# Reordering the opening and the projection stage of a depool and feed-forward kernel

## What is computed

```python
h = rmsnorm(layernorm(x), g_res) @ W_in.T + b_in
c = rmsnorm(ctx, g_init)[:, :512]                # the mean square is over all 1024 columns
s[t] = a * s[t-1] + b * c[t]                     # a scan over the 3202 rows, a = 1 - exp(-0.001)
plug = clip(cumsum(boundary(cumsum(mask))) - 1, 0, 3201)
x1 = x + h + s[plug]
out = x1 + gelu(layernorm(x1) @ w1 + b1) @ w2 + b2    # w1 is 512 x 2048, w2 is 2048 x 512
```

## Time and profile before

| what | value |
|---|---|
| median of 3 runs (lowest to highest) | 852.49 us (850.71 to 853.28) |
| the profiled execution, its own time | 856.67 us |
| its span | 854.9 us |
| mean granted TensorE clock | 0.994 |
| TensorE matmuls busy | 835.0 us, 98% |
| VectorE, ScalarE, POOL busy | 322.9, 273.9, 251.5 us |
| chain that ended last | 90% TensorE, 3% VectorE, 2% ScalarE, 2% DMA |
| POOL, four low parts of w1 (128x512 each, L487, at 114.37) | 5.61 us |
| VectorE CAST of 128x26 at 43.40, beside a POOL product; another at 47.96, alone | 1.29 us, 0.18 us |

### The profile page before, as it was taken

The page is one execution under the profiler, slowest core; times in us unless marked ns, Lnnn a source line. Parts: engine busy times, 40 slices in busy tenths (PEclk is TensorE's granted clock), DMA queues, the critical chain, the costliest instruction groups (busy, mean ns, idle before and its releaser), DMA issues.

```text
span 854.9 us, 10715 instructions
## 1 busy us (share of the span) xinstructions
PE 835.0 (98%) x3766; PEld 683.4 (80%) x3766; DVE 322.9 (38%) x529; ACT 273.9 (32%) x482; POOL 251.5 (29%) x234
## 2 busy tenths in 40 slices
PE   5899999899999999999999999999999999999998
PEld 3688888688888888788888887888888888888886
DVE  4899972434333241424141424234113411241112
ACT  4173325542441235122622243213222222222221
POOL 0174176970163106220532034202500250011000
PEclk9899999999999999999999999999999999999999
DMA  9567698150213212150116021402300140010001
GB/s 241 173 177 241 208 257 308 50 155 17 74 49 108 63 50 74 51 119 9 64 68 151 0 74 49 97 0 74 74 1 1 49 87 11 0 49 1 1 1 49
DMA packets 34968, 71.07 MB, mean 83 GB/s; under 512 B 5716, under 2 KB 5716, under 8 KB 33176
## 3 DMA queue, kind: packets, MB, share of 16 engines
q1 hardware_dynamic: 25964, 58.91, 21.2%
q0 software_dynamic: 4608, 8.39, 6.1%
q10 hardware_dynamic: 4368, 3.42, 1.4%
HBM read 47.87 MB, written 22.84 MB: 83 GB/s over the span
## 4 chain that ended last, share of the span: by engine, by line
PE 90%; DVE 3%; ACT 2%; issue 2%; DMA 2%; POOL 0%; ACTq 0%; SPq 0%; DVEq 0%; POOLq 0%
PE acc L781 15%; PE acc L783 15%; PE acc L782 15%; PE h_bank L781 14%; PE h_bank L782 14%; PE h_bank L783 14%; PE t_bank L827 2%; DVE cl L949 2%; PE t_bank L769 1%; DMA ch<-in_ctx_dram 1%; PE acc L777 1%; DMA xa_even<-in_x_dram 1%; PE t_bank L800 1%; PE acc L769 0%; ACT g_f L721 0%
## 5 line engine op out<-in xcount | busy, mean ns | idle before, releaser
L1155 DVE TENSOR_TENSOR h_lo<-g_f,h_hi 128x512 fp32r<-128x512 f32 x128 | 99.6, 778 | 456.1 <-ACT g_f L721 456.1
L719 ACT ACTIVATE h_hi<-h_bank,b_c 128x512 fp32r<-128x512 f32 x128 | 88.1, 688 | 436.9 <-PE h_bank L783 432.0
L781 PE MATMUL h_bank<-xt_hi,w_hi 128*128 128x512 f32 x512 | 202.4, 395 | 0.0
L783 PE MATMUL h_bank<-xt_hi,w_lo 128*128 128x512 f32 x512 | 200.0, 391 | 0.0
L782 PE MATMUL h_bank<-xt_lo,w_hi 128*128 128x512 f32 x512 | 200.0, 391 | 0.0
L781 PE MATMUL acc<-w_hi,h_hi 128*128 128x512 f32 x512 | 199.8, 390 | 0.0
L783 PE MATMUL acc<-w_hi,h_lo 128*128 128x512 f32 x512 | 199.2, 389 | 0.0
L782 PE MATMUL acc<-w_lo,h_hi 128*128 128x512 f32 x512 | 199.2, 389 | 0.0
L781 PEld LDWEIGHTS h_bank<-xt_hi,w_hi 128*128 128x128 f32 x512 | 96.6, 189 | 21.0 <-issue 1.2
L782 PEld LDWEIGHTS h_bank<-xt_lo,w_hi 128*128 128x128 f32 x512 | 96.4, 188 | 20.9 <-issue 1.2
L783 PEld LDWEIGHTS h_bank<-xt_hi,w_lo 128*128 128x128 f32 x512 | 96.5, 189 | 20.3
(11 more groups left out here) (152 smaller groups left out, 687.8 us busy)
## 6 DMA issues: line engine op xcount, KB each, us to landing
out_dram<-x_cur SPq DMA_DIRECT2D x32, 256.0 KB, 2.1
x_next<-x_part SPq DMA_DIRECT2D x7, 1024.0 KB, 4.8
w_raw<-in_L_ffn_w_dram SPq DMA_DIRECT2D x6, 1024.0 KB, 9.8
scan_table<-cl SPq DMA_DIRECT2D x6, 896.0 KB
ch<-in_ctx_dram SPq DMA_DIRECT2D x20, 256.0 KB, 2.9
cl<-in_ctx_dram SPq DMA_DIRECT2D x5, 1024.0 KB
xa_even<-in_x_dram SPq DMA_DIRECT2D x16, 256.0 KB, 5.8
xa_odd<-in_x_dram SPq DMA_DIRECT2D x16, 256.0 KB, 6.7
```

Of the source, the lines that this page charges most:

```text
L719: act.activation(h_hi[:, m % HB, :], h_bank[m % 2][:], ACT.Gelu, bias=b1_c[:, m:m + 1])
L781: nc.tensor.matmul(dst, a_hi, b_hi, start=first, stop=False)
L783: return nc.tensor.matmul(dst, a_lo, b_hi, start=False, stop=final)
L1155: dve.tensor_tensor(h_lo[:, m % HB, :], g_f32[:], h_hi[:, m % HB, :].bitcast(F32), ALU.subtract).then_inc(h_split, 1)
```

## The change

- TensorE first makes 20 transposes of the identity into a bank nobody reads (`warm_up`). The sums over W_in are issued k by k: two, then the transposes of tile 0, then two.
- The first three tiles are projected with k as the outer loop: k = 0 and 1 for tiles 0 and 1, then for tile 2, the transposes of tile 3, k = 2 and 3 for the three tiles, the transposes of tile 4. The loop goes on with tile 3.
- The low parts of W_in for k = 2 and 3 are made by POOL, ahead of its first `scales` and behind its constants.
- ScalarE takes the high parts of tiles 1, 2 and 3 between those of W_in, VectorE the low parts of tiles 1, 2 and 3 likewise; statistics run four tiles ahead (LEAD), not six, with two per step at t = 22 to 24; POOL makes scales at t = 3, 7, ..., 23 and 24.
- The steps of the mask, the scans, the carries and the stores of blocks 0 and 1 come one or two tiles later; `count_rows` is one tile ahead of `count_before`, before it was two.
- For block 2, the first two high rows are loaded at t = 18, the low rows at t = 26, the other two high rows behind the tile loop and ahead of the last 4 MB of weights; its squares are made at t = 28 and 29 and at m = 0 and 1 of group 0. In group 0 POOL's low parts of the second quarter of w2 come behind block 2's products and scales.

```diff
+WARM = 20
+LEAD = 4
@@ SP
-                if t == 19:
-                    store_block(0, cl)
-                if t == 21:
-                    store_block(1, cl_next)
-                if t == 27:
-                    wait_apart(sp, table_stored, STORED + BLOCK_STORED * 2)
+                if t == 18:
                     load_high_half(NA, 0)
                     load_high_half(NA, 1)
+                if t == 20:
+                    store_block(0, cl)
+                if t == 22:
+                    store_block(1, cl_next)
+                if t == 26:
+                    wait_apart(sp, table_stored, STORED + BLOCK_STORED * 2)
                     load_low_half(NA)
                 if t == 29:
                     load_w1(1)
                     load_w2(1)
+            load_high_half(NA, 2)
+            load_high_half(NA, 3)
             store_x1(NT - 1)
@@ POOL
-            scales(0, 2)
-            scales(2, 2)
             for q in range(HP):
                 band_part(q)
             pool.sem_inc(consts_made, 1)
+            for k in (2, 3):
+                pool.wait_ge(win_hi_done, k + 1)
+                pool.tensor_tensor(win_lo[:, k, :], win_raw[:, k, :], win_hi[:, k, :].bitcast(F32),
+                                   ALU.subtract).then_inc(win_lo_late, 1)
+            scales(0, 2)
+            scales(2, 2)
...
-                if t % 4 == 2 and t + 2 < NT:
-                    scales(t + 2, TI)
+                if t % TI == TI - 1 and t < 24:
+                    scales(t + 1, TI)
+                if t == 24:
+                    scales(28, TI)
...
-                    for q in range(4):
-                        low_w2(1, q, 4)
                 if scan:
                     for j in range(R):
                         times_g_init(NA + g, j, cl)
                     context_scale(NA + g, ss_h, ss_l, rc)
+                if first:
+                    for q in range(4):
+                        low_w2(1, q, 4)
@@ ScalarE
-            tile_high(0)
-            for k in range(K):
+            tile_high(0)
+            tile_high(1)
+            high_w_in(0)
+            high_w_in(1)
+            tile_high(2)
+            high_w_in(2)
+            high_w_in(3)
+            tile_high(3)
...
+                if t in (28, 29):
+                    if t == 28:
+                        act.wait_ge(cl_loaded, 16 * (NA + 1))
+                    act.wait_ge(ch_loaded[t - 28], 16)
+                    squares(t - 28, ch[:, t - 28, :], cl, ss_h, ss_l)
...
+                    if first and m in (0, 1):
+                        act.wait_ge(ch_loaded[m], 16 * 2)
+                        squares(2 + m, ch[:, m, :], cl, ss_h, ss_l)
@@ TensorE
+            def project_first_part(t, k):
+                pe.wait_ge(x_lo, t + 1)
+                if k < 2:
+                    pe.wait_ge(win_lo_done, k + 1)
+                else:
+                    pe.wait_ge(win_lo_late, k - 1)
+                project_part(t, k)
+
+            def warm_up():
+                for _ in range(WARM):
+                    nc.tensor.transpose(acc[0][:, 0:P], ident[:], ident[:])
...
+            warm_up()
+            sum_w_in(0)
+            sum_w_in(1)
             transpose_first(0)
-            sum_w_in()
+            sum_w_in(2)
+            sum_w_in(3)
             transpose_first(1)
-            for t in range(NT):
+            transpose_first(2)
+            for k in (0, 1):
+                project_first_part(0, k)
+                project_first_part(1, k)
+            project_first_part(2, 0)
+            project_first_part(2, 1)
+            transpose_first(3)
+            for k in (2, 3):
+                for t in range(3):
+                    project_first_part(t, k)
+            transpose_first(4)
+            for t in range(3, NT):
                 if t + 2 < NT:
                     transpose_first(t + 2)
-                if t == 2:
+                if t == 4:
                     mask_totals()
-                if t == 12:
+                if t == 14:
                     count_positions()
-                if t == 14:
+                if t == 16:
                     count_before()
-                if t == 15:
                     pe.wait_ge(consts_made, 5)
                     carry(0, cl, acc[3][:])
-                if t == 18:
+                if t == 19:
@@ VectorE
-            tile_stats(0)
             tile_low(0)
             centre_w_in(0)
             centre_w_in(1)
+            tile_low(1)
             low_w_in(0)
             centre_w_in(2)
             low_w_in(1)
             centre_w_in(3)
-            low_w_in(2)
-            low_w_in(3)
-            tile_low(1)
-            for t in range(1, 6):
-                tile_stats(t)
+            tile_low(2)
+            tile_stats(0)
+            tile_stats(1)
+            tile_low(3)
+            tile_stats(2)
+            tile_stats(3)
...
-                if t < 20:
-                    tile_stats(t + 6)
-                elif t < 23:
-                    tile_stats(26 + 2 * (t - 20))
-                    tile_stats(27 + 2 * (t - 20))
+                if t < 22:
+                    tile_stats(t + LEAD)
+                elif t < 25:
+                    tile_stats(2 * t - 18)
+                    tile_stats(2 * t - 17)
```

More of the change, by code:

```diff
@@ L275, in xattn_ffn @@
         win_lo_done = sem("win_lo_done")
+        win_lo_late = sem("win_lo_late")
         mv_a_ready = sem("mv_a_ready")
@@ L420, in group @@
             def group(g, scan, more, prep):
-                if scan:
-                    b = NA + g
+                b = NA + g
+                if scan and not isinstance(g, int):
                     load_high_half(b, 2)
@@ L437, in group @@
                     sp.dma_start(out_v[g, :, i, :], x_cur[:, i, :]).then_inc(out_stored, 16)
-            with sp.Fori(0, NB - NA - 1) as g:
+            group(0, True, True, True)
+            with sp.Fori(1, NB - NA - 1) as g:
                 group(g, True, True, True)
+            load_high_half(NB - 1, 2)
+            load_high_half(NB - 1, 3)
             group(NB - NA - 1, True, False, True)
@@ L673, in _ @@
                           allow_slow_non_contiguous=True).then_inc(small_loaded, 16)
-            tile_high(1)
             for t in range(NT):
-                if t + 2 < NT:
+                if 2 <= t < NT - 2:
                     tile_high(t + 2)
@@ L725, in group @@
                         high_w2(1)
-                    if scan and first <= m <= 2 + first:
+                    if scan and not first and m <= 2:
                         b = NA + g
-                        for j in ((0, 1), (2,), (3,))[m - first]:
+                        for j in ((0, 1), (2,), (3,))[m]:
                             act.wait_ge(ch_loaded[j % 2], 16 * (2 * g + j // 2 + 1))
@@ L770, in transpose_first, with sum_w_in @@
                 ins.then_inc(x_turned, 1)
[L772 to L778, removed]
+            def sum_w_in(k):
+                pe.wait_ge(g_made, k + 1)
+                pe.wait_ge(win_loaded[k], 16)
+                ins = nc.tensor.matmul(acc[3][:], g_wide[:, k, :], win_raw[:, k, :], start=(k == 0), stop=(k == K - 1))
+                if k == K - 1:
+                    ins.then_inc(win_summed, 1)
             def split_product(dst, a_hi, a_lo, b_hi, b_lo, first, final):
@@ L789, in project, with project_part @@
                 for k in range(K):
[L790 to L796, removed]
+                    project_part(t, k)
+            def project_part(t, k):
+                c = slice(k * P, (k + 1) * P)
+                ins = split_product(p_bank[t % 3][:], h_hi[:, t % HB, c], h_lo[:, t % HB, c],
+                                    win_hi[:, k, :], win_lo[:, k, :], k == 0, k == K - 1)
+                if k == K - 1:
+                    ins.then_inc(h_used, 1)
+            def project_first_part(t, k):
[4 more added lines that the diff above has]
+                    pe.wait_ge(win_lo_late, k - 1)
+                project_part(t, k)
+            def warm_up():
+                for _ in range(WARM):
+                    nc.tensor.transpose(acc[0][:, 0:P], ident[:], ident[:])
             def carry(b, rows, dst):
@@ L1088, in _ @@
                     tile_add(t - 1)
-                if t + 2 < NT:
+                if 2 <= t < NT - 2:
                     tile_low(t + 2)
-                if t == 0:
+                if t == 1:
                     mask_parts()
-                if t == 3:
+                if t == 5:
                     mask_positions()
-                if t == 4:
+                if t == 6:
                     mask_carries()
-                if t == 5:
+                if t == 7:
                     mask_places()
-                if t == 6:
+                if t == 8:
@@ L1100, in _ @@
                     mask_rows()
-                if t == 7:
+                if t == 9:
                     one_hots_q()
-                if t == 8:
+                if t == 10:
                     one_hots_p(0, MJ // 2)
```

(16 more changed lines are left out.)

5 lines of the change are left out of this document (3 added, 2 removed).

## The result

The changed kernel takes 854.80 us (median of 13 runs, 853.48 to 856.62), the kernel before beside it 852.68 (13 runs): ratio 1.0025, 95% interval 1.0016 to 1.0035. The forecast was 846.3 and a gain of 0.7%; it is a small loss, outside the range. The two profiled executions have the same span, 854.9 us.

What follows compares the result with a forecast made beforehand. TensorE was taken as the bound, VectorE as a hidden second one. On the profiled 856.67 us, -3.7 + 1.7 - 4.2 = -6.2; with that execution's 4.2 over the median kept, 846.3 us, range 841.0 to 850.4.

Steps and rivals of the forecast that it cites:

- Warm-up and sums: Opening: transposes raise TensorE's clock at 8.3 us; sums over W_in end at 11.65, 2.85 earlier than 14.50.
- The wait for the row totals: TensorE waits about 3 us for the mask's second row totals, now one tile ahead, not two.
- VectorE as the second bound: Tile loop: VectorE's queue is almost without pause for 83.4 us, so TensorE's lead can't be kept whole.
- Block 2: Earlier loads and squares: scans run 157.7 to 162.9, the carry is wanted at 163.65, its 2.48 us wait goes.
- Rival 2: Opening: transposes warm nothing, clock rises at 12.9, sums run to about 13.8; 848.4 us; chance 0.08.
- Rival 4: Tail: late statistics hold the gathers, last statistics after 111 us; slower, 855 us; chance 0.05.
- the landing of the gathers: Tail: fourth gather issued at 111.1 takes 5.4 us, landing at 116.5, or 118.0 as the other end.
- the step from the profiled execution to the median: Profiled execution (856.67) is 4.2 us above the median of 852.49; that difference is taken over unchanged.
- VectorE's line: VectorE's queue to the last statistics: 86.2 us of work from 16.2, a 1.2 wait, ending at 103.6.
- -3.7: Tail: normed rows come at 119.2, so the feed-forward stage starts 3.7 us earlier than before.
- +1.7: Clock lost behind TensorE's 3 us wait at t = 30: 1.7 us, ends 0 and 3.4.
- -4.2: Block 2's carry: the 2.48 us wait and 1.7 of clock go, 4.2 us won; ends 0 and 4.2.

Runs made afterwards that it cites:

- block2_only: Kernel before with only block 2's part of the change (loads, squares, POOL's low halves of w2): 854.02 us, 1.0014.
- b2_early: Kernel before with block 2's part of the change, but the low rows loaded at t = 21, between the stores of blocks 0 and 1: 853.57 us, 1.0012.
- best2: Changed kernel, gathers before last scales, low rows loaded at t = 28, second-norm scales before POOL's w1 low halves, counts at t = 17: 848.74 us.
- best3: Changed kernel, gathers before last scales, low rows loaded at t = 28, counts at t = 17, w1 low halves as in the change: 846.71 us, 0.9925.
- open_only: The change without its part on block 2 (loads, squares and low halves of w2 as before): 857.02 us, 1.0047.
- open_late: The change without its part on block 2, with block 2's 1.5 MB load at t = 28 in place of t = 27: 852.83 us, 0.9996.
- after: The changed kernel itself, against the kernel before: 854.80 us, 1.0025.
- warm0: Changed kernel without its 20 warm-up transposes (WARM = 0): 856.58 us, 1.0043.
- cl_early: Changed kernel with block 2's low rows (1 MB) loaded at t = 22, ahead of the gathers: 851.01 us, 0.9981.
- cl_late: Changed kernel with block 2's low rows loaded at t = 28, behind the gathers, and first two squares at t = 30 and 31: 849.65 us, 0.9968.
- gathers_first: Changed kernel with POOL issuing the four gathers ahead of the scales of tiles 28 to 31: 850.95 us, 0.9988.

## Why the prediction was wrong

**Right, by its own steps.** Warm-up and sums: 11.49 for 11.65, with the clock up at about 8.2 for 8.3; that it should rise 5.6 to 6.0 us after the first work is borne out less well, since two traces of the old opening have 3.1 and 3.3. Tile 3 at 23.94 for 24.1. The wait for the row totals 2.2 for 3. VectorE as the second bound: of the lead of 10.6 us at tile 3, the last statistics show 0.5. Block 2: the scans run from 162.6, which is on time, since TensorE comes to the carry 4.7 us later than before, and the carry waits 0.2. Rival 2, by which transposes do not warm, is ruled out by the run without them. Rival 4 has the measured time (855), but by luck: it asks for last statistics behind 111 us, and they came at 105.3. The page of the Trainium skill named there, TensorE: Matmul & The Clock Gate, "Part 4: PE-mode transpose", says that the upper clock does not engage for transpose-mode. For fp32 transposes by an identity this case contradicts it: with twenty of them ahead of the sums the rise came at about 8.2 us in place of 12.4.

**The step that failed** is the landing of the gathers: "That load is split up now (high rows at t = 18, low rows at t = 26, about 105), so I take 5.4, near the median: 116.5, and 118.0 as the other end." I had explained the 6.9 us of one gather by a load issued near it, and then moved a load of 1 MB among the four, took the median of the three figures, and as the worst end the price of a load issued behind all of them. No end covered a load issued ahead of them. It was issued at 109.0, not at 105, and the three gathers behind it landed in 9.2 to 10.3. The mean share of the DMA engines would not have told it: from 109 to 120 it is 0.96 here and was 0.94 before. What tells the cases apart is the order of issue: gathers issued from 0.6 us ahead of the load to 3.9 us behind it take 9.1 to 10.6 us, those at least 1.4 us ahead of it or over 9 us behind it 4.8 to 6.9. Why a load ahead costs so much more than one behind is not shown.

Three terms were mis-sized besides, the third being the step from the profiled execution to the median. VectorE's line ended at 105.34, not 103.6: started 0.3 earlier and with a wait of 1.48 for 1.2, it holds 88.0 us of work where I summed 86.2. Three small operations met POOL's products, one each in the positions, carries and rows (1.07, 1.27 and 1.20 us where 0.2 is their price), where before one did so (1.29). And the clock: behind the wait of 5.3 us the lower level held from 124.4 to 131.3, of which 5.5 us with TensorE at work, 2.8 lost in place of 1.7.

In the terms of the sum, for the profiled executions: -3.7 became +2.3 (6.0 more: 1.7 us from the later statistics, 3.8 from the landing, some 0.5 from VectorE's order behind it), +1.7 became +2.8, and -4.2 held. That makes +0.9, and the spans are equal; the 0.9 left over is not accounted for, but for 0.4 us of small waits at the carry that are gone too.

**The profiled execution was not a usual one.** "That execution is 4.2 us above the median of 852.49; I take the difference over unchanged" was the third: the profiled execution of after lies only 1.8 us above its median, and the other 2.4 us turn equal spans into the loss that the medians show. The terms had been read from an execution with about 10 us at the lower clock (granted clock 0.994). Beside the experiments the kernel before ran 94 times: 62 times with a granted clock of 0.998 or more, which is at most some 3.4 us at the lower level, and a median of 851.8, and 32 times with 0.996 or less and a median of 854.5. The changed kernel had 0.994 to 0.996 in all of its 13.

Two traces show where the difference sits. `block2_only` and `b2_early` are the kernel before up to t = 18, and their profiled executions lie at their medians:

```profile
103.66 0.18 DVE L946 BATCH_NORM_AGGREGATE mv_a<-st_a 128x2 f32<-128x6 f32 x1
105.55 1.81 POOL L525 DMA_INDIRECT x_next<-scan_table,idx  x1 [0.19 <-issue]
```

In them the sums over W_in end at 13.49 and 13.07, not at 14.50; the same gap ahead of the mask totals (3.27 us) costs 3.4 us at the lower clock, not 6.8; and the last statistics come at 103.66 (the first row, `block2_only`) and 103.25, not at 105.65. In eight traces with the new opening and its warm-up and LEAD of 4 they come at 103.6 to 105.2 (`best2` and `best3`, with the counts moved, at 102.8 and 103.1). So, as far as these two traces stand for the usual execution, the new opening does not bring the last statistics forward at all, and the gathers neither (the first at 105.55 in the second row, at 105.7 to 107.0 with the new opening where they stand behind the scales): VectorE's queue had eaten the whole lead. Block 2 is alike. `open_only` and `open_late`, with block 2 as before, wait 2.3 and 2.4 us at the carry and keep the upper clock behind it; the 4.2 us that the forecast took off are what it cost in one execution, which, with its wait of 2.1 us at t = 30, is why `block2_only` gained nothing in its timed runs.

**What stays open.** Which of its waits cost clock in the other executions of the kernel before isn't on record. The clock behind a given wait differs between executions: the wait of 2.2 us for the row totals was followed by some 3.4 us at the lower level in four traces (`after`, `warm0`, `cl_early`, `cl_late`) and by none in five. The cost of a load of 1 MB against a gather of the same size, other than by the places of it tried here, was not measured either.

## What to carry to other kernels

A lead that one engine wins drags along every queue whose waits hang on it, here the one that issues loads, while what hangs on another engine stays: ask of each pair of transfers, now apart, whether they meet. A duration measured when a transfer was alone, or ahead of its neighbour, is no price for one behind it, and the mean share of the DMA engines does not show the difference. And look at what the chain to the next stage hangs on before giving its first link (here the last statistics, ahead of the gathers in an in-order queue) away for slack elsewhere. Last, a profile is one execution: compare its time and granted clock with those of the timed runs before taking a wait and its clock for what a change can win.

## What the runs showed of the hardware

Four indirect gathers of 256 KB with an add, issued 1.9 us apart, landed in 4.8 to 6.9 us each when they were issued 1.4 us or more ahead of a plain load of 1 MB or over 9 us behind it, and in 9.1 to 10.6 when issued from 0.6 us ahead of it to 3.9 us behind it (`after`, `warm0`, `gathers_first`, `open_only`, `block2_only`). With such a load issued right ahead of a store of 0.9 MB, the gathers that wait for this store started 4.0 us later in one case (106.3 for 102.3) and 3.4 in the other (108.9 for 105.5).

Twenty fp32 transposes of 128x128 count towards the upper clock. From TensorE's first matmul to the rise passed 3.1 to 6.1 us in four traces without them, two of them of the same opening with 3.1 and 6.0. A gap of 3.3 us was followed by 3.4 or by 6.8 us at the lower clock, one of 2.2 us by 3.4 or by nothing.

Beside a running POOL product, VectorE's norms (128x512, from SBUF to SBUF) took 1.4 to 1.5 us in place of 0.54, and some operations of 26 and 78 columns 1.07 to 1.29 in place of 0.2; statistics kept their 0.66 to 0.69, and adds and splits that read PSUM their 0.75 and 0.68.
